# Rotated attention: transposes and values one pair later behind the scores

## The chip, the cores and the metric

The kernel runs on one core of one Trainium2 chip. Its engines are TensorE (PE, with its weight loads PEld), VectorE (DVE), ScalarE (ACT), GpSimd (POOL) and SyncE (SP, which starts the transfers). The metric is the time of one execution on the device in microseconds, lower is better; it is given as the median of three runs.

## The reference, cut to what matters

The program is a decoder: an attention layer with rotated queries and keys (stage A), a cross attention, a gated layer, six layers of linear attention, another cross attention, and six layers (stage F) of rotated local attention followed by a gated layer. The change touches the rotated local attention alone, in stage A and in the six layers of stage F. There are 2 batches of 512 tokens, 16 heads of 64, and each query sees itself and the 32 tokens before it.

```python
# stage F, one layer; stage A is the same without l2norm, scales and QK_SCALE
q = l2norm(q) * qs
k = l2norm(k) * ksc
q = q * cos * scale + rotate_half(q) * sin * scale
k = k * cos * inv + rotate_half(k) * sin * inv
mask = (it < jb) | (it > jb + w) | (jb == -1)
sim = jnp.einsum('bhwie,bhwje->bhwij', bq, bk2) * QK_SCALE
sim = jnp.where(mask, -jnp.finfo(sim.dtype).max, sim)
attn = jax.nn.softmax(sim, -1)
out = jnp.einsum('bhwij,bhwje->bhwie', attn, bv2)
return out @ Wo
```

## The kernel before, in words

Every engine has its own program, written out by hand in the order in which it is to run, and semaphores tie them. One batch of rotated attention has two parts. The first makes the projections of queries, keys and values; DVE multiplies them with the rotation's tables, SP swaps halves by a transfer, and POOL adds the two products (L559, L560). The second goes over the 8 pairs of heads, and this is where the change is. In what follows a step p is one turn of the loop over pairs on PE.

In step p PE does, in this order: a wait for the query, for the key and for both differences of pair p - 1, whose scores stand in the same two banks of PSUM; in stage F alone the spread of the norms of pair p + 1 over the partitions (L324, two matmuls); the mask (L345, for the last pair of stage F L340) and the scores (L353, 16 matmuls); the transposes of the probabilities of pair p - 1 (L367, four for each head, each head behind its own wait for POOL); and the values of pair p - 2 (L384). At step 8 the output products of pairs 0 to 3 (L394) stand ahead of the last transposes, later those of 4, 5 and of 6, 7. In steps 0 and 1 one value projection each (L276) stands among them.

DVE does for each pair the norm product of the next query (L507), the maximum of both heads (L527), the difference (L530), the sum of the exponentials (L538) and its reciprocal (L541); behind the last pair it adds the output to x (L545). ACT takes the exponential (L471), copies the norms of the next key (L455), the transposes (L478) and the values (L483). POOL multiplies the next key with its norms (L552, in stage F from pair 2 on) and then scales the probabilities with the reciprocal (L567), in the order L552 of p + 1, L567 of p, L552 of p + 2.

Probabilities lie in P, one buffer for each head and two pairs; the differences in shft, likewise; the transposes in PT, likewise. P is set to zero ahead of stage A (L1735) and ahead of stage F (L1636), since the transposes read a few columns that the exponential doesn't write. In batch 1 of a layer of stage F the parts of the next token shift and norm stand between the pairs: L1594 and L1595 on DVE behind pair 1, L1515 on PE in step 2, L1604 on DVE behind pair 3, L1188 on PE in step 4.

Of the kernel before, what the change touches and what calls it, by code (L numbers as in the profile page):

```python
# [21 lines left out]
ALU = mybir.AluOpType  # L22
ACT = mybir.ActivationFunctionType
AX = mybir.AxisListType.X
# [71 lines left out]
def build(nc, A, out, book):  # L96
    Signal.every = []
    nc.disable_value_cache = True
    with ExitStack() as c:
# [65 lines left out]
        def read(eng, bank, sgn, key):  # L165

            eng.wait_ge(*sgn.at(key))
            eng.sem_inc(free[bank].mark()[0], 1)
# [47 lines left out]
        tmp = ar(3, 2, T)  # L216
        sinp = ar(3, 2 * T)
        swp = ar(3, 2 * T)
        shft = ar(4, 384)
        P = ar(4, 640)  # L220
        PT = ar(4, 512)
        rn = rs[:, 1, :]
        knr = ar(2, T)
        ssel = ar(4, 32)
        spr = ar(4, 128)
        scl = ar(2)
# [31 lines left out]
            eng.wait_ge(swapped[n % 3], Loop.reg * per + (per + at) if Loop.now else at)  # L258

        FIRST = 2  # L260

        def k_full(key, b, p, l2):

# [2 lines left out]
        def blocks(v):  # L266
            return v.rearrange("p (j k) -> p j k", j=4)[:, :, 0:KW]
# [90 lines left out]
        def a_turn_pe(pe, key, b, p):  # L358
            for h in range(2):
                pe.wait_ge(*scaled.at((key, b, p, h)))  # L360
                if p == 0:
                    take(pe, 4 + h)
                else:
                    pe.wait_ge(*turned.at((key, b, p - 1, h)))
                for j in range(4):
                    at0 = 160 * j - (WIN if j % 2 else 0)
                    last = pe.transpose(ps[:, 4 + h, 128 * j:128 * j + 128], P[:, 2 * (p % 2) + h, at0:at0 + 128], ident[:, :])  # L367
                last.then_inc(*full[4 + h].mark((key, b, "t", p)))

        def a_values_pe(pe, key, b, p):  # L370
# [27 lines left out]
        def attn_pe(pe, key, src, l2, between={}):  # L398
            for b in range(B):
                a_proj_pe(pe, key, b, src(b), l2)  # L400
                if l2:
                    a_spread_pe(pe, key, b, 0)
                for p in range(NP + 2):
                    if p < 2:
                        a_v_pe(pe, key, b, src(b), NT + 2 + p)
                    if p < NP:
                        a_scores_wait(pe, key, b, p, l2)
                    if l2 and p + 1 < NP:
                        a_spread_pe(pe, key, b, p + 1)
                    if p < NP:  # L410
                        a_scores_pe(pe, key, b, p, l2)
                    if b == 1 and p in between:
                        between[p]()
                    if p == NP:
                        a_out_pe(pe, key, b, range(0, 4))
                    if 1 <= p <= NP:
                        a_turn_pe(pe, key, b, p - 1)
                    if p >= 2:
                        a_values_pe(pe, key, b, p - 2)
                    if p == NP:  # L420
                        a_out_pe(pe, key, b, range(4, 6))
                a_out_pe(pe, key, b, range(6, NP))

# [35 lines left out]
        def attn_act(act, key, l2, between={}):  # L459
            for b in range(B):  # L460
                a_proj_act(act, key, b, l2)
                for p in range(NP + 2):
                    if p < 2:
                        a_v_act(act, key, b, NT + 2 + p)
                    if l2 and FIRST <= p + 1 < NP:
                        a_k_norm_act(act, key, b, p + 1)
                    if p < NP:
                        for h in range(2):
                            i = 2 * (p % 2) + h
                            act.wait_ge(*subbed.at((key, b, p, h)))  # L470
                            act.activation(blocks(P[:, i, :]), shft[:, i, :].rearrange("p (j k) -> p j k", j=4), ACT.Exp,  # L471
                                           scale=8.0 if l2 else D ** -0.5).then_inc(*exped.mark((key, b, p, h)))
                    if 1 <= p <= NP:
                        for h in range(2):
                            act.wait_ge(*full[4 + h].at((key, b, "t", p - 1)))
                            if p >= 3:
                                act.wait_ge(*full[6].at((key, b, "o", p - 3)))
                            act.activation(PT[:, 2 * ((p - 1) % 2) + h, :], ps[:, 4 + h, :], ACT.Copy).then_inc(*turned.mark((key, b, p - 1, h)))  # L478
                            if p == NP:
                                read(act, 4 + h, turned, (key, b, p - 1, h))  # L480
                    if p >= 2:
                        act.wait_ge(*full[6].at((key, b, "o", p - 2)))
                        act.activation(OT[:, p - 2, :], ps[:, 6, :], ACT.Copy).then_inc(*merged.mark((key, b, p - 2)))  # L483
                        if p == NP + 1:
                            read(act, 6, merged, (key, b, p - 2))
                    if b == 1 and p in between:
                        between[p]()

# [26 lines left out]
        def attn_dve(dve, key, l2, between={}):  # L515
            for b in range(B):
                a_proj_dve(dve, key, b, l2)
                if l2:
                    a_q_norm_dve(dve, key, b, 0)
                for p in range(NP):  # L520
                    if l2 and p + 1 < NP:
                        a_q_norm_dve(dve, key, b, p + 1)
                    s4 = lambda h: ps[:, h, 0:4 * KW].rearrange("p (j k) -> p j k", j=4)
                    i = p % 3
                    for h in range(2):
                        dve.wait_ge(*full[h].at((key, b, "s", p)))
                        dve.tensor_reduce(nm[:, i, 4 * h:4 * h + 4], s4(h), AX, ALU.max).then_inc(*topped.mark((key, b, p, h)))  # L527
                    for h in range(2):
                        dve.wait_ge(*topped.at((key, b, p, h)))
                        dve.tensor_tensor(shft[:, 2 * (p % 2) + h, :].rearrange("p (j k) -> p j k", j=4), s4(h),  # L530
                                          nm[:, i, 4 * h:4 * h + 4].unsqueeze(2).to_broadcast([128, 4, KW]), ALU.subtract)\
                            .then_inc(*subbed.mark((key, b, p, h)))
                    if p == NP - 1:
                        for h in range(2):
                            read(dve, h, subbed, (key, b, p, h))
                    for h in range(2):
                        dve.wait_ge(*exped.at((key, b, p, h)))
                        dve.tensor_reduce(nm[:, i, 8 + 4 * h:12 + 4 * h], blocks(P[:, 2 * (p % 2) + h, :]), AX, ALU.add)\  # L538
                            .then_inc(*added.mark((key, b, p, h)))
                    dve.wait_ge(*added.at((key, b, p, 1)))  # L540
                    dve.reciprocal(nm[:, i, 16:24], nm[:, i, 8:16]).then_inc(*inverted.mark((key, b, p)))  # L541
                    if b == 1 and p in between:
                        between[p]()
                dve.wait_ge(*full[3].at((key, b, "y")))
                dve.tensor_tensor(x[:, T * b:T * b + T], x[:, T * b:T * b + T], ps[:, 3, :], ALU.add)\  # L545
                    .then_inc(*x_new.mark((key, b)))
                read(dve, 3, x_new, (key, b))
# [6 lines left out]
        def attn_pool(pool, key, l2):  # L554
            for b in range(B):
                for p in range(NP):
                    i = slot(b, p)
                    swap_wait(pool, b, p)
                    pool.tensor_tensor(Q[:, p, :], tmp[:, i, 0, :], swp[:, i, 0:T], ALU.add).then_inc(*roped.mark((key, b, p)))  # L559
                    pool.tensor_tensor(KT[:, p, :], tmp[:, i, 1, :], swp[:, i, T:2 * T], ALU.add).then_inc(*k_added.mark((key, b, p)))  # L560
                for p in range(NP):
                    if l2 and FIRST <= p + 1 < NP:
                        a_k_raise_pool(pool, key, b, p + 1)
                    pool.wait_ge(*inverted.at((key, b, p)))
                    for h in range(2):
                        v = blocks(P[:, 2 * (p % 2) + h, :])
                        pool.tensor_tensor(v, v, nm[:, p % 3, 16 + 4 * h:20 + 4 * h].unsqueeze(2).to_broadcast([128, 4, KW]), ALU.mult)\  # L567
                            .then_inc(*scaled.mark((key, b, p, h)))
                pool.wait_ge(*scaled.at((key, b, NP - 1, 1)))
# [37 lines left out]


        fix = sb("fix", [128, 3400])
        fat = [0]  # L610

        def keep(*dims):
# [1266 lines left out]
```

## Time and profile before

| | |
|---|---|
| median of 3 runs | 2211.46 us (2206.73 to 2217.43) |
| the profiled execution | 2206.81 us |
| its span | 2205.0 us |
| PE busy | 1757.6 us, 80% |
| DVE busy | 1332.5 us, 60% |
| ACT busy | 887.0 us, 40% |
| POOL busy | 552.3 us, 25% |
| mean granted TensorE clock | 0.881 |

The span goes from the first to the last instruction. Busy time is a mean over stages with different limits; the row of one instruction group says how long one of them took and, behind the bar, how long its engine idled ahead of it and what released it. Matmuls overlap, so the distance between the starts of two rows says more than their length. The granted clock is the share of TensorE's full speed: 1.00 is 2.4 GHz, 0.50 is 1.2 GHz.

### The profile page before, as it was taken

The numbers are of one execution on the slowest core, as the hardware profiler recorded it, in microseconds if no ns is written. First come the engines' busy times: TensorE is split into PE (matmuls) and PEld (weight loads), VectorE is DVE, ScalarE is ACT, GpSimd is POOL, SyncE is SP. The second block draws the span as 40 slices with busy tenths as digits, with TensorE's granted clock in tenths as the row PEclk, the third lists the DMA queues.
The fourth block names the chain that finished last, engine by engine and source line by source line (L and its number), as shares of the span: only waits on it lengthen the run. The fifth ranks groups of instructions, "written<-read, shape, count | busy, mean of one in ns | idle before, by whom it ended". The sixth has DMA issues, their size and how long they took to land.

```text
span 2205.0 us, 44619 instructions
## 1 busy us (share of the span) xinstructions
PE 1757.6 (80%) x15573; PEld 935.4 (42%) x15573; DVE 1332.5 (60%) x2278; ACT 887.0 (40%) x1529; POOL 552.3 (25%) x524
## 2 busy tenths in 40 slices
PE   6883331588887988886769989998988989998998
PEld 2552110254554636452225444453552543544544
DVE  6655577473544636353357748657666775685774
ACT  2341110224132241423235555454555554555545
POOL 3440000000000000000015516534543462461652
PEclk9996555698888798987779999999999999999999
DMA  5110000000000000000032313313214123132230
GB/s 201 54 59 0 0 0 0 21 6 13 7 11 8 11 17 1 17 1 0 1 113 65 104 51 104 104 40 114 79 38 140 47 62 127 27 104 82 72 104 11
DMA packets 48288, 111.26 MB, mean 50 GB/s; under 512 B 15024, under 2 KB 17840, under 8 KB 46896
## 3 DMA queue, kind: packets, MB, share of 16 engines
q1 hardware_dynamic: 48048, 108.00, 14.8%
q8 instruction: 157, 2.57, 0.5%
q14 instruction: 83, 0.68, 0.1%
HBM read 28.54 MB, written 0.52 MB: 13 GB/s over the span
## 4 chain that ended last, share of the span: by engine, by line
issue 63%; PE 17%; POOL 12%; DVE 4%; ACT 2%; DMA 1%; POOLq 0%; DVEq 0%; ACTq 0%; SPq 0%
POOL big L567 4%; POOL big L559 3%; POOL big L560 3%; PE ps L394 3%; POOL big L552 2%; PE ps L287 2%; PE ps L292 2%; PE ps L384 2%; PE ps L324 2%; PE ps L367 1%; PE ps L310 1%; PE ps L276 1%; DVE big L530 1%; PE ps L353 1%; DMA big<-big 1%
## 5 line engine op out<-in xcount | busy, mean ns | idle before, releaser
L559 POOL TENSOR_TENSOR big<-big 128x512 f32<-128x512 f32 x112 | 142.6, 1273 | 1390.3 <-DMA big<-big 1389.4
L567 POOL TENSOR_TENSOR big<-big,nm 128x384 f32<-128x384 f32 x224 | 184.3, 844 | 217.1 <-DVE nm L541 217.1
L471 ACT ACTIVATE big<-big 128x384 f32<-128x384 f32 x224 | 110.3, 523 | 211.2 <-DVE big L530 210.7
L500 DVE TENSOR_TENSOR big<-ps,big 128x512 f32<-128x512 f32 x224 | 153.5, 685 | 43.0 <-POOL big L560 26.3
L367 PE MATMUL ps<-ident,big 128*128 128x128 f32 x896 | 143.2, 294 | 30.0 <-POOL big L567 20.8
L501 DVE TENSOR_TENSOR big<-ps,big 128x512 f32<-128x512 f32 x224 | 152.1, 679 | 0.0
L560 POOL TENSOR_TENSOR big<-big 128x512 f32<-128x512 f32 x112 | 142.8, 1275 | 0.0
L324 PE MATMUL ps<-rs,big 32*128 32x512 f32 x384 | 109.9, 648 | 41.0 <-DVE big L530 20.4
L478 ACT ACTIVATE big<-ps 128x512 f32<-128x512 f32 x224 | 121.5, 585 | 50.8 <-PE ps L367 47.3
L527 DVE TENSOR_REDUCE nm<-ps 128x4 f32<-128x384 f32 x224 | 113.8, 549 | 40.4 <-PE ps L353 40.1
L1399 DVE TENSOR_TENSOR big<-ps,fix 128x512 f32<-128x512 f32 x192 | 119.4, 683 | 29.7 <-PE ps L1147 25.8
L1147 PE MATMUL ps<-big 32*128 32x128 f32 x1536 | 114.0, 340 | 27.1 <-DVE big L1399 15.6
L367 PEld LDWEIGHTS ps<-ident,big 128*128 128x128 f32 x896 | 103.8, 148 | 74.1 <-issue 49.5
L1278 ACT ACTIVATE sq<-xc 128x512 f32<-128x512 f32 x36 | 22.7, 629 | 276.4 <-DVE xc L1422 274.4
L384 PE MATMUL ps<-big 128*64 128x64 f32 x3584 | 129.0, 225 | 0.0
L1147 PEld LDWEIGHTS ps<-big 32*128 32x128 f32 x1536 | 101.4, 236 | 57.4 <-DVE big L1399 24.1
L384 PEld LDWEIGHTS ps<-big 128*64 128x64 f32 x3584 | 113.5, 138 | 27.2 <-issue 27.2
L538 DVE TENSOR_REDUCE nm<-big 128x4 f32<-128x384 f32 x224 | 113.8, 549 | 16.0 <-ACT big L471 4.1
L287 PE MATMUL ps<-xsh,big 128*128 128x512 f32 x192 | 104.1, 625 | 21.1 <-issue 15.0
L530 DVE TENSOR_TENSOR big<-ps,nm 128x384 f32<-128x384 f32 x224 | 113.2, 546 | 0.0
L427 ACT ACTIVATE big<-ps 128x512 f32<-128x512 f32 x112 | 65.1, 592 | 111.6 <-PE ps L276 111.6
L394 PE MATMUL ps<-big 128*128 128x512 f32 x224 | 107.4, 612 | 0.0
(245 smaller groups left out, 3163.9 us busy)
## 6 DMA issues: line engine op xcount, KB each, us to landing
big<-big SPq DMA_DIRECT2D x224, 256.0 KB, 2.4
big<-big SPq DMA_DIRECT2D x112, 128.0 KB, 2.4
big<-in_F_w SPq DMA_DIRECT2D x6, 1536.0 KB, 6.0
big<-big SPq DMA_DIRECT2D x84, 64.0 KB, 2.0
big<-in_D_w SPq DMA_DIRECT2D x18, 256.0 KB, 2.7
big<-in_F_wo SPq DMA_DIRECT2D x6, 512.0 KB, 7.1
big<-in_F_w SPq DMA_DIRECT2D x6, 341.0 KB, 3.0
big<-in_A_w SPq DMA_DIRECT2D x1, 1536.0 KB, 9.8
```

The costliest lines, as they stand in the source:

```text
L287: pe.matmul(ps[:, kq, :], Wqkv[:, 0, 128 * p:128 * p + 128], src, start=True, stop=True).then_inc(*full[kq].mark((key, b, "q", p)))
L324: pe.matmul(ps[:, k, :], spr[r:r + 32, p // 2, :], rn[r:r + 32, :], start=True, stop=True, tile_position=(r, 0))\
L367: last = pe.transpose(ps[:, 4 + h, 128 * j:128 * j + 128], P[:, 2 * (p % 2) + h, at0:at0 + 128], ident[:, :])
L384: last = pe.matmul(ps[64 * h:64 * h + 64, 6, 64 * m:64 * m + 64], vv[:, m // 2, 128 * p + 64 * h:128 * p + 64 * h + 64], PT[:, 2 * (p % 2) ...
L394: last = pe.matmul(ps[:, 3, :], Wo[:, p, :], OT[:, p, :], start=p == 0, stop=p == NP - 1)
L500: dve.tensor_tensor(tmp[:, i, w, :], ps[:, k, :], tb[:, 2 * w, :], ALU.mult).then_inc(*part.mark((key, b, p, 0)))
L501: dve.tensor_tensor(sinp[:, i, T * w:T * w + T], ps[:, k, :], tb[:, 2 * w + 1, :], ALU.mult).then_inc(*part.mark((key, b, p, 1)))
L530: dve.tensor_tensor(shft[:, 2 * (p % 2) + h, :].rearrange("p (j k) -> p j k", j=4), s4(h), nm[:, i, 4 * h:4 * h + 4].unsqueeze(2).to_broad ...
L559: pool.tensor_tensor(Q[:, p, :], tmp[:, i, 0, :], swp[:, i, 0:T], ALU.add).then_inc(*roped.mark((key, b, p)))
L560: pool.tensor_tensor(KT[:, p, :], tmp[:, i, 1, :], swp[:, i, T:2 * T], ALU.add).then_inc(*k_added.mark((key, b, p)))
L567: pool.tensor_tensor(v, v, nm[:, p % 3, 16 + 4 * h:20 + 4 * h].unsqueeze(2).to_broadcast([128, 4, KW]), ALU.mult)\
L1147: last = pe.matmul(ps[:, r, 128 * gp:128 * gp + 128], Kz[rows, b, gp, sl], Qf[rows, b, gp // 2, sl], start=True, stop=True, tile_position= ...
```

## The change

The transposes of pair p - 2 and the values of pair p - 3 now stand in step p, where those of p - 1 and p - 2 stood, on PE and with them the copies on ACT. The loop has one turn more. P has buffers for three pairs, shft for one. The norm copy knr lies in an unused part of another tensor, fix, so that the buffers fit. Nothing else is computed, and no transfer is changed.

```diff
-        shft = ar(4, 384)
-        P = ar(4, 640)
+        shft = ar(2, 384)
+        P = ar(6, 640)
         PT = ar(4, 512)
         rn = rs[:, 1, :]
-        knr = ar(2, T)
...
+        LATE = 2
...
-                for p in range(NP + 2):
+                for p in range(NP + LATE + 1):
...
-                    if 1 <= p <= NP:
-                        a_turn_pe(pe, key, b, p - 1)
-                    if p >= 2:
-                        a_values_pe(pe, key, b, p - 2)
-                    if p == NP:
+                    if LATE <= p < NP + LATE:
+                        a_turn_pe(pe, key, b, p - LATE)
+                    if p > LATE:
+                        a_values_pe(pe, key, b, p - LATE - 1)
+                    if p == NP + 1:
                         a_out_pe(pe, key, b, range(4, 6))
...
-                            i = 2 * (p % 2) + h
                             act.wait_ge(*subbed.at((key, b, p, h)))
-                            act.activation(blocks(P[:, i, :]), shft[:, i, :].rearrange("p (j k) -> p j k", j=4), ACT.Exp,
+                            act.activation(blocks(P[:, 2 * (p % 3) + h, :]), shft[:, h, :].rearrange("p (j k) -> p j k", j=4), ACT.Exp,
...
+        knr = fix[:, N:2 * N].rearrange("p (i t) -> p i t", i=2)
```

On PE, at the start of the pairs of stage A, batch 0, before (L345 and L353 are mask and scores of a pair, L276 a value projection, L367 transposes, L384 values):

```order
L276 MATMUL ps<-big,xn 128x512
L345 MATMUL ps<-band,identb 64x384 x4
L353 MATMUL ps<-big 64x64 x2
L353 MATMUL ps<-big 64x96 x14
L367 MATMUL ps<-ident,big 128x128 x8
L345 MATMUL ps<-band,identb 64x384 x4
L353 MATMUL ps<-big 64x64 x2
L353 MATMUL ps<-big 64x96 x14
L367 MATMUL ps<-ident,big 128x128 x8
L384 MATMUL ps<-big 64x64 x16
```

The same place in the changed kernel:

```order
L276 MATMUL ps<-big,xn 128x512
L345 MATMUL ps<-band,identb 64x384 x4
L353 MATMUL ps<-big 64x64 x2
L353 MATMUL ps<-big 64x96 x14
L345 MATMUL ps<-band,identb 64x384 x4
L353 MATMUL ps<-big 64x64 x2
L353 MATMUL ps<-big 64x96 x14
L367 MATMUL ps<-ident,big 128x128 x8
```

The scores of pair 2 have moved ahead of the first transposes, and the first values one step back. In stage F the same happens, with L324 ahead of each mask.

On PE, behind the last scores of that batch, in the changed kernel (L394 are output products, L287 is the next batch's first projection):

```order
L384 MATMUL ps<-big 64x64 x16
L394 MATMUL ps<-big 128x512 x4
L367 MATMUL ps<-ident,big 128x128 x8
L384 MATMUL ps<-big 64x64 x16
L367 MATMUL ps<-ident,big 128x128 x8
L384 MATMUL ps<-big 64x64 x16
L394 MATMUL ps<-big 128x512 x2
L384 MATMUL ps<-big 64x64 x16
L394 MATMUL ps<-big 128x512 x2
L287 MATMUL ps<-xn,big 128x512
```

Before, one group of L367 and one of L384 stood between the first and the second L394; now there are two of each.

## Rows read from the trace of the kernel before

**Rows 1.** The page's first line.
```profile
span 2205.0 us, 44619 instructions
```

**Rows 2.** Groups by line: busy, mean ns, idle before and its releaser.
```profile
L545 DVE TENSOR_TENSOR x<-x,ps 128x512 f32<-128x512 f32 x14 | 9.6, 688 | 142.8 <-PE ps L394 142.8
```

**Rows 3.** Timeline, PE, stage F mid-batch: start, us, engine, line, operation, idle before.
```profile
1720.78 1.13 PE L324 MATMUL ps<-rs,big 32*128 32x512 f32 x4
...
1724.23 1.15 PE L384 MATMUL ps<-big 128*64 128x64 f32 x32
...
1729.70 1.13 PE L324 MATMUL ps<-rs,big 32*128 32x512 f32 x4
```

**Rows 4.** Timeline, PE, the same batch behind its last pair.
```profile
1734.24 0.50 PE L340 MATMUL ps<-bandw,identb 128*128 128x384 bf16 x2
...
1736.18 1.43 PE L367 MATMUL ps<-ident,big 128*128 128x128 f32 x8 [0.62 <-POOL big L567]
...
1738.62 3.70 PE L394 MATMUL ps<-big 128*128 128x512 f32 x8
1742.16 1.04 PE L367 MATMUL ps<-ident,big 128*128 128x128 f32 x8
1743.13 1.15 PE L384 MATMUL ps<-big 128*64 128x64 f32 x32
1744.21 1.98 PE L394 MATMUL ps<-big 128*128 128x512 f32 x4
```

**Rows 5.** Timeline, all engines, steps 1 and 2 of a batch at full clock.
```profile
1534.84 1.27 POOL L552 TENSOR_TENSOR big<-big 128x512 f32<-128x512 f32 x1
1535.09 1.01 DVE L530 TENSOR_TENSOR big<-ps,nm 128x384 f32<-128x384 f32 x2
...
1536.52 1.13 PE L324 MATMUL ps<-rs,big 32*128 32x512 f32 x4 [0.86 <-POOL big L552]
...
1537.56 1.61 POOL L567 TENSOR_TENSOR big<-big,nm 128x384 f32<-128x384 f32 x2 [1.45 <-DVE nm L541]
...
1539.57 1.01 DVE L530 TENSOR_TENSOR big<-ps,nm 128x384 f32<-128x384 f32 x2
```

**Rows 6.** Timeline, a spread that waited for DVE alone.
```profile
1710.52 1.01 DVE L530 TENSOR_TENSOR big<-ps,nm 128x384 f32<-128x384 f32 x2
...
1711.76 1.23 PE L324 MATMUL ps<-rs,big 32*128 32x512 f32 x4 [0.31 <-DVE big L530]
```

**Rows 7.** Windows: busy of PE, PEld, DVE, ACT, POOL; PEclk; DMA share, GB/s.
```profile
1706.00:1709.00 3.00, 1.92 (x34) 1.15 (x38) 2.76 (x6) 2.07 (x4) 0.69 (x1) 0.93 0.07 18
1709.00:1712.00 3.00, 2.69 (x24) 2.08 (x18) 2.29 (x5) 0.90 (x3) 2.15 (x3) 0.50 0.21 44
1432.00:1435.00 3.00, 3.00 (x40) 1.43 (x36) 2.52 (x5) 1.36 (x3) 2.31 (x3) 0.50 0.02 5
```

**Rows 8.** Timeline, PE, spread and scores at half clock.
```profile
1431.49 2.08 PE L324 MATMUL ps<-rs,big 32*128 32x512 f32 x4 [0.33 <-DVE big L530]
...
1433.81 1.49 PE L353 MATMUL ps<-big 64*64 64x64 f32 x32
```

**Rows 9.** Timeline, stage A, batch 0: PE and DVE.
```profile
57.08 1.97 PE L367 MATMUL ps<-ident,big 128*128 128x128 f32 x8 [4.35 <-POOL big L567]
58.98 0.54 PE L345 MATMUL ps<-band,identb 64*64 64x384 bf16 x4
...
60.49 1.02 DVE L527 TENSOR_REDUCE nm<-ps 128x4 f32<-128x384 f32 x2 [4.35 <-PE ps L353]
...
63.73 0.97 DVE L527 TENSOR_REDUCE nm<-ps 128x4 f32<-128x384 f32 x2
...
82.82 3.70 PE L394 MATMUL ps<-big 128*128 128x512 f32 x8
```

**Rows 10.** Timeline, the start: zeroing of P, and the first norm.
```profile
1.36 2.19 DVE L1735 MEMSET big<- 128x2560 f32 x1 [1.36 <-PEq L1873]
...
7.97 0.69 DVE L185 TENSOR_TENSOR xc<-x,ps 128x512 f32<-128x512 f32 x1
```

More of the change, by code:

```diff
@@ L366, in a_turn_pe @@
                     at0 = 160 * j - (WIN if j % 2 else 0)
-                    last = pe.transpose(ps[:, 4 + h, 128 * j:128 * j + 128], P[:, 2 * (p % 2) + h, at0:at0 + 128], ident[:, :])
+                    last = pe.transpose(ps[:, 4 + h, 128 * j:128 * j + 128], P[:, 2 * (p % 3) + h, at0:at0 + 128], ident[:, :])
                 last.then_inc(*full[4 + h].mark((key, b, "t", p)))
@@ L461, in attn_act @@
                 a_proj_act(act, key, b, l2)
-                for p in range(NP + 2):
+                for p in range(NP + LATE + 1):
                     if p < 2:
@@ L468, in attn_act @@
                         for h in range(2):
-                            i = 2 * (p % 2) + h
                             act.wait_ge(*subbed.at((key, b, p, h)))
-                            act.activation(blocks(P[:, i, :]), shft[:, i, :].rearrange("p (j k) -> p j k", j=4), ACT.Exp,
+                            act.activation(blocks(P[:, 2 * (p % 3) + h, :]), shft[:, h, :].rearrange("p (j k) -> p j k", j=4), ACT.Exp,
                                            scale=8.0 if l2 else D ** -0.5).then_inc(*exped.mark((key, b, p, h)))
-                    if 1 <= p <= NP:
+                    i = p - LATE
+                    if 0 <= i < NP:
                         for h in range(2):
[L475 to L485, printed above, removed]
+                            act.wait_ge(*full[4 + h].at((key, b, "t", i)))
+                            if i >= 2:
+                                act.wait_ge(*full[6].at((key, b, "o", i - 2)))
+                            act.activation(PT[:, 2 * (i % 2) + h, :], ps[:, 4 + h, :], ACT.Copy).then_inc(*turned.mark((key, b, i, h)))
+                            if i == NP - 1:
+                                read(act, 4 + h, turned, (key, b, i, h))
+                    if i >= 1:
+                        act.wait_ge(*full[6].at((key, b, "o", i - 1)))
+                        act.activation(OT[:, i - 1, :], ps[:, 6, :], ACT.Copy).then_inc(*merged.mark((key, b, i - 1)))
+                        if i == NP:
+                            read(act, 6, merged, (key, b, i - 1))
                     if b == 1 and p in between:
@@ L529, in attn_dve @@
                         dve.wait_ge(*topped.at((key, b, p, h)))
-                        dve.tensor_tensor(shft[:, 2 * (p % 2) + h, :].rearrange("p (j k) -> p j k", j=4), s4(h),
+                        dve.tensor_tensor(shft[:, h, :].rearrange("p (j k) -> p j k", j=4), s4(h),
                                           nm[:, i, 4 * h:4 * h + 4].unsqueeze(2).to_broadcast([128, 4, KW]), ALU.subtract)\
@@ L537, in attn_dve @@
                         dve.wait_ge(*exped.at((key, b, p, h)))
-                        dve.tensor_reduce(nm[:, i, 8 + 4 * h:12 + 4 * h], blocks(P[:, 2 * (p % 2) + h, :]), AX, ALU.add)\
+                        dve.tensor_reduce(nm[:, i, 8 + 4 * h:12 + 4 * h], blocks(P[:, 2 * (p % 3) + h, :]), AX, ALU.add)\
                             .then_inc(*added.mark((key, b, p, h)))
@@ L565, in attn_pool @@
                     for h in range(2):
-                        v = blocks(P[:, 2 * (p % 2) + h, :])
+                        v = blocks(P[:, 2 * (p % 3) + h, :])
                         pool.tensor_tensor(v, v, nm[:, p % 3, 16 + 4 * h:20 + 4 * h].unsqueeze(2).to_broadcast([128, 4, KW]), ALU.mult)\
```

## The prediction

> **What bounds the kernel now.** I read, in this order, the page, the list of instruction groups, the timeline of one layer of stage F, the same stretch in the other batches, the timeline of stage A, and the granted clock in short windows. The edit touches only the rotated attention: stage A and the six layers of stage F, two batches each, so 14 batches of 8 pairs, inside a span of 2205.0 us (the execution itself took 2206.81) [rows 1].
>
> A pair of heads costs a step. In F it is, on PE, the spread of the norms (L324), the mask and the scores (L345, L353), the transposes (L367) and the values (L384); on DVE the norm product, maximum, difference, sum and reciprocal; on POOL the scaling of the probabilities (L567) and the k product (L552). In mid-batch PE runs without a gap: two steps take 1729.70 - 1720.78 = 8.92 us, and the values end just where the next L324 starts [rows 3]. Of the 8.92 about 0.4 is PE standing between the two heads' transposes, since POOL has not yet scaled the second head. So PE is the bound by a hair, with a wait on POOL in it. Behind the last pair PE waits 0.62 for POOL before the transposes of pair 6, and then runs a tail with no gap at all: output products, transposes, values, output products [rows 4]. The reader should see that DVE has nothing to do in that tail: its addition L545 waits 142.8 us in 14 batches for the last L394, 10.2 each [rows 2]. Whatever is added to the tail is paid in full.
>
> In A there is no norm and no k product. POOL is still busy with the rotations when the first probabilities are there, so PE waits 4.35 us before the first transposes, and DVE waits as long for the third pair's scores, which stand behind those transposes on PE [rows 9]. Later steps alternate between short ones and ones with a 1.2 us wait for POOL.
>
> **The change part by part.**
>
> *The tail.* Transposes of pair p - 2 and values of p - 3 now stand at step p. After the last scores PE has one set of transposes and one of values more to do. They cost 1743.13 - 1742.16 = 0.97 and 1744.21 - 1743.13 = 1.08 [rows 4], together 2.05 per batch. No wait existed there that they could fill (the one at 1736.18 stands ahead of the tail). They come out of steps 1 and 2, where PE was waiting for DVE anyway. Bounds: 2.05 whole, or 1.4 if the copies on ACT hid a part. I take 2.05.
>
> *Steps in F, batch 0.* With the transposes one step later POOL's scaling is no longer waited for directly, and PE needs 1.06 + 0.95 + 0.97 + 1.08 = 4.06 per step. What is late next? First DVE: from the start of a spread to the end of the differences is 1539.57 + 1.01 - 1536.52 = 4.06 [rows 5], and from there to the next spread 1711.76 - 1711.53 = 0.23 [rows 6]: 4.29 a step, 8.58 for two. Second POOL, which is not relieved: the k product of pair p + 1 still stands behind the scaling of pair p - 1. From the end of the differences (1536.10) the scaling starts 1.46 later, takes 1.57 to the start of L552, L552 takes 1.27, and PE starts 0.41 after its end (1536.11 to 1536.52) [rows 5]. That is 4.71, and with 4.06 on it, 8.77 for two steps. So two steps go from 8.92 to 8.77 and not to 8.58: 0.3 over four steps, and 0.2 at the last, where no spread is needed. After the last scores 1738.62 - 1734.24 = 4.38 [rows 4] becomes 1.32 for mask and scores, 0.97 and 1.08: 3.37, 1.0 less. Batch 0: -0.3 - 0.2 - 1.0 + 2.05 = +0.55.
>
> *Steps in F, batch 1.* The work put between its pairs (token shift, mean, variance, root) holds the steps open on DVE and ACT and stays. I take -0.3 (between 0 and the 0.5 of batch 0) and -0.8 after the last scores: +0.95. Six layers: 6 x (0.55 + 0.95) = +9.0; bounds +4 (all steps at 8.58) and +12 (no step shorter).
>
> *Stage A.* Scores of pair 2 now stand ahead of the first transposes. These start at 57.08 as before, for POOL's rotations are unchanged; behind them, at 58.98, come scores 3 instead of 2. From there to the output products it was 82.82 - 58.98 = 23.84. Now there are four steps at DVE's pace of 63.73 - 60.49 = 3.24 [rows 9], 3.0 for the last scores, transposes and values, and I add 1.0 for a slow clock at the start: 17.0, so -6.8, and +2.05 for the tail: -4.8 a batch, -9.6 for both. Bounds -13 and -5.
>
> *The buffers.* P grows from 4 to 6 times 640 columns. It is zeroed twice, on DVE, ahead of a norm that waits for it: the 2560 columns took 2.19, and L185 starts as soon as the zeroing is over [rows 10]. Half as much again is 1.1, twice: +2.2. One difference buffer per head costs nothing: DVE's sum of pair p - 1 has already waited for the exponential that reads it. Three buffers of P are enough, as ACT reaches the exponential of p after it copied the transposes of p - 3. The norm copy on a borrowed place in another tensor moves no instruction. No DMA moves, and SP's and POOL's queues keep their order. On ACT the copies of the transposes (L478) and of the values (L483) move with PE's work, still behind the exponential of their step, so no new wait stands ahead of an exponential.
>
> *The clock.* At the end of step 0 in F PE idles 1.40 us, as in all 12 batches, and in 8 of the 12 F batches the granted clock then falls from 1.00 (2.4 GHz) to 0.50 (1.2 GHz) in step 1; it stays there for three or four microseconds, in one batch for about ten [rows 7, 8]. In step 1 the slow transposes partly fill a gap, so a fall costs 0.3 to 1.0 us, 3.2 in the long one; over 12 batches 8 us, 0.67 each. The change takes the transposes out of step 1 and the values out of step 2. PE then idles about 2.3 us in step 1 (4.29 less 2.0 of spread and scores) and 1.3 in step 2. A clock that often fell after 1.40 will nearly always fall after both, and the slow stretch will lie on the spread and scores of step 2, which DVE waits for: 1.13 becomes 2.08 and 0.83 becomes 1.49 [rows 8], +1.6 to +1.8 a batch. Net of the 0.67 I take +1.1 x 12 = +13. Bounds: 0 (no more falls than now), and +30 if most batches do what the long one did.
>
> The Trainium skill, page "TensorE: Matmul & The Clock Gate", section "What's actually happening", says that the throttled state is the default and that activity releases it. By that rule work taken out of a thin stretch is paid again in clock, and the sum would be the one above; without it, it would be 13 less. The trace agrees: full clock through the dense tail, half clock after thin steps.
>
> **The sum.** +9.0 - 9.6 + 2.2 + 13 = +14.6 on the profiled 2206.81: 2221.4. The median of the runs, 2211.46, stands 4.65 above the profiled execution, so by it the forecast is 2226; I say 2225.
>
> **The rivals.**
> *Clock unchanged.* The falls of the clock stay at 8 in 12 with the same price. For it: four batches hold full clock through the same 1.40. Against: the gap grows. +9.0 - 9.6 + 2.2 = +1.6, 2213.
> *Faster: no waits, no falls.* The extra step of lead keeps PE from waiting on POOL, steps follow each other at DVE's 4.29, and the work ahead in A and F closes the thin stretch, so that the clock no longer falls. Then F is +4, A -13, the buffers +2.2, and the 8 us of clock come back: -15, 2197. It decides in step 1 of each F batch: no granted clock under 1.00 there. Against it stands that instructions leave this step.
> *Long falls.* PE, idle in the slow stretch too, does not get its clock back at once, and most batches look like the one at 1429 [rows 7]. Clock +28: 2240.
> *The lead does not work*, because something holds scores 2 behind the first transposes in A (a buffer of P or of the differences). Then A gives nothing, and the time is about 2235 with the clock's term. The buffers argue against it.
>
> **Chances.** Forecast 0.50, clock unchanged 0.25, long falls 0.12, no lead 0.05, faster 0.08. About 0.5% (11 us) is what a measurement of this kernel can tell from no change. Slower by more than that: most of the forecast (0.39; its own range, 2217 to 2233, reaches under 2222.5), long falls and no lead, 0.56. Faster 0.07. Same 0.37. The range is 2203 to 2239: from the clock-unchanged case with A at its best to the long falls.
>
> **What would show it.** Right: L394 starts about 5 us sooner against the first scores in A, the stretch from the first L394 to L545 is 2.05 longer in all 14 batches, two mid-batch steps take 8.8, the zeroing of P takes 3.3, and windows of 0.50 stand in steps 1 to 2 of nearly every F batch. Wrong: full clock in those steps, or a tail that did not grow, or steps at 8.6, or a first transposes' start in A other than 57 + 1.1.

## The result, and the profile after

The changed kernel takes 2227.55 us (median of 8 runs, 2222.19 to 2235.71). The kernel before, on the same chip, takes 2208.98 us (8 runs, 2199.77 to 2217.43). The ratio is 1.0085, with a 95% interval of 1.0058 to 1.0112: slower by about 0.85%. Here and in the experiments the ratio and its interval are worked out over all the runs, and are not the quotient of the two medians. The forecast was 2225 us, and its likeliest side was slower.

The profiled execution took 2223.19 us, 16.38 more than the one before; the spans differ by 16.4, so all of it can be looked for in the trace. The page of the changed kernel, its first lines (compare [rows 1]; PE was busy for 1757.6 us before, and the mean granted clock falls from 0.881 to 0.864):

```profile
span 2221.4 us, 44619 instructions
...
PE 1763.4 (79%) x15573; PEld 944.6 (43%) x15573; DVE 1335.4 (60%) x2278; ACT 891.3 (40%) x1529; POOL 553.5 (25%) x524
```

The same instructions, and yet PE is busy for 5.8 us more. The groups of the kernel before (busy us, mean ns, then the idle time ahead of them and what ended it):

```profile
L367 PE MATMUL ps<-ident,big 128*128 128x128 f32 x896 | 143.2, 294 | 30.0 <-POOL big L567 20.8
...
L324 PE MATMUL ps<-rs,big 32*128 32x512 f32 x384 | 109.9, 648 | 41.0 <-DVE big L530 20.4 <-DVE big L513 8.2 <-ACT rs L447 7.9
```

and of the changed kernel, with the addition that answers to [rows 2]:

```profile
L367 PE MATMUL ps<-ident,big 128*128 128x128 f32 x896 | 131.4, 294 | 1.1 <-POOL big L567 0.9
...
L324 PE MATMUL ps<-rs,big 32*128 32x512 f32 x384 | 123.4, 721 | 68.1 <-DVE big L530 27.7 <-POOL big L552 19.3 <-DVE big L513 8.1
...
L545 DVE TENSOR_TENSOR x<-x,ps 128x512 f32<-128x512 f32 x14 | 9.6, 688 | 158.3 <-PE ps L394 158.3
```

Three things are seen. The wait of the transposes for POOL is gone, 30.0 us down to 1.1. The wait ahead of the spread L324 has grown by 27.1 us. Its waits for DVE's difference grew by 7.3, and POOL's k product, which was not among the three largest before (so under 7.9), now ends 19.3 of it. That the two sums are nearly equal does not mean that one wait has moved: 21.3 of the 27.1 lie in one place, ahead of the third spread of each batch of F, where step 1 ends. It waited 0.31 to 0.89 us before and waits 2.21 to 2.42 now, in 8 of the 12 batches for POOL's k product (8 x 2.41 is the 19.3), in the others for DVE's difference. One of the eight:

```profile
1245.45 2.08 PE L324 MATMUL ps<-rs,big 32*128 32x512 f32 x4 [2.41 <-POOL big L552]
```

And the mean spread takes 721 ns instead of 648: the same matmuls at a lower clock. The addition behind each batch waits 15.5 us more in 14 batches. That is 1.1 a batch, and not 2.05, since the idle time ahead of L545 starts only where DVE's last work of the batch ends.

From there the span can be taken apart by the starts of a few instructions. Each row is a stretch; the numbers are from the two traces:

| stretch | before | after | difference |
|---|---|---|---|
| start to first scores of A | 48.24 | 48.48 | +0.24 |
| first scores of A to the second L545 | 112.88 | 103.14 | -9.74 |
| stages in between, up to the zeroing for F | 957.80 | 955.68 | -2.12 |
| the zeroing for F, up to the norm | 8.13 | 9.46 | +1.33 |
| norm to the first scores of F | 44.81 | 44.80 | -0.01 |
| first scores of F to the last L545 | 1006.71 | 1033.38 | +26.67 |
| last L545 to the end | 26.43 | 26.46 | +0.03 |

Stage F loses 26.7, A gives back 9.7. Within F the 12 batches, each from its first mask to L545, were summed in three pieces: the loop up to the last mask 386.9 to 400.8 (+13.9), from there to the first L394 51.3 to 40.2 (-11.1), from the first L394 to L545 127.2 to 152.5 (+25.3).

The slow clock is seen at once in a batch of F. Windows of the changed kernel (columns as in [rows 7]), over steps 0 to 3 of the batch that begins at 1524.83:

```profile
1525.00:1528.00 3.00, 1.90 (x38) 0.94 (x31) 3.00 (x6) 0.36 (x1) 0.69 (x1) 1.00 0.48 107
1528.00:1531.00 3.00, 2.28 (x40) 1.21 (x40) 2.37 (x6) 1.71 (x4) 1.47 (x2) 0.84 0.21 44
1531.00:1534.00 3.00, 1.22 (x4) 0.51 (x4) 2.78 (x7) 0.99 (x2) 1.37 (x2) 0.50 0.00 0
1534.00:1537.00 3.00, 3.00 (x41) 1.91 (x39) 1.05 (x2) 0.60 (x1) 2.88 (x3) 0.50 0.00 0
1537.00:1540.00 3.00, 2.69 (x12) 1.61 (x10) 2.81 (x7) 1.84 (x4) 0.00 (x0) 0.50 0.03 5
1540.00:1543.00 3.00, 3.00 (x42) 1.87 (x39) 1.02 (x2) 0.72 (x2) 2.81 (x3) 0.50 0.00 0
```

PEclk, the granted clock and the third value from the end of each line, falls in step 1 and is 0.50 in the last four windows, that is for at least 12 us. In the kernel before the same batch held 1.00 through all its steps, though it had the same idle 1.40 us ahead of the second spread (a row and the window around it):

```profile
1532.04 1.13 PE L324 MATMUL ps<-rs,big 32*128 32x512 f32 x4 [1.40 <-DVE big L530]
```

```profile
1531.00:1534.00 3.00, 1.96 (x40) 1.11 (x40) 2.72 (x6) 2.07 (x4) 0.73 (x1) 1.00 0.09 22
```

The place of the fall in the changed kernel, in the timeline of PE and DVE (start, us, engine, line, and in brackets the idle time before):

```profile
1528.30 1.13 PE L324 MATMUL ps<-rs,big 32*128 32x512 f32 x4 [1.40 <-DVE big L530]
...
1529.55 1.03 PE L353 MATMUL ps<-big 64*64 64x64 f32 x32
...
1532.78 2.08 PE L324 MATMUL ps<-rs,big 32*128 32x512 f32 x4 [2.21 <-DVE big L530]
...
1534.88 0.69 DVE L507 TENSOR_TENSOR big<-big,ps 128x512 f32<-128x512 f32 x1 [0.95 <-PE ps L324]
...
1535.11 1.49 PE L353 MATMUL ps<-big 64*64 64x64 f32 x32
...
1536.64 1.02 DVE L527 TENSOR_REDUCE nm<-ps 128x4 f32<-128x384 f32 x2 [1.07 <-PE ps L353]
...
1538.82 2.08 PE L324 MATMUL ps<-rs,big 32*128 32x512 f32 x4 [0.31 <-DVE big L530]
```

The gap that was 1.40 is followed by a new one of 2.21, because nothing but spread and scores is left in step 1 (before, 0.86 us were idle there). The spread that ends it runs at half clock, and DVE, which sets the pace here, waits for it twice: 0.95 us ahead of the norm product, 1.07 ahead of the maximum. So this step takes 1538.82 - 1532.78 = 6.04 us. At full clock it takes 4.29 to 4.38 (experiment 3).

The tail of the same batch, which answers to [rows 4]:

```profile
1558.10 0.50 PE L340 MATMUL ps<-bandw,identb 128*128 128x384 bf16 x2
...
1561.45 3.70 PE L394 MATMUL ps<-big 128*128 128x512 f32 x8
1564.99 1.04 PE L367 MATMUL ps<-ident,big 128*128 128x128 f32 x8
1565.96 1.15 PE L384 MATMUL ps<-big 128*64 128x64 f32 x32
1567.04 1.09 PE L367 MATMUL ps<-ident,big 128*128 128x128 f32 x8
1568.06 1.15 PE L384 MATMUL ps<-big 128*64 128x64 f32 x32
1569.14 1.98 PE L394 MATMUL ps<-big 128*128 128x512 f32 x4
```

From the first to the second L394 it is now 7.69 us; before, it was 5.59. No gap, so the additional pair is paid in full. In front of it, from the last mask to the first L394, 3.35 instead of 4.38.

Stage A, batch 0, which answers to [rows 9]:

```profile
55.15 0.36 PE L345 MATMUL ps<-band,identb 64*64 64x384 bf16 x4 [2.18 <-DVE big L530]
...
57.44 1.97 PE L367 MATMUL ps<-ident,big 128*128 128x128 f32 x8 [0.75 <-POOL big L567]
59.34 0.53 PE L345 MATMUL ps<-band,identb 64*64 64x384 bf16 x4
...
66.91 0.36 PE L345 MATMUL ps<-band,identb 64*64 64x384 bf16 x4
...
70.10 0.36 PE L345 MATMUL ps<-band,identb 64*64 64x384 bf16 x4
...
76.47 3.70 PE L394 MATMUL ps<-big 128*128 128x512 f32 x8
```

The scores of pair 2 stand ahead of the first transposes, PE waits 0.75 us for POOL instead of 4.35, and the output products begin at 76.47 instead of 82.82. The steps have DVE's pace, 70.10 - 66.91 = 3.19.

The start, which answers to [rows 10]:

```profile
1.62 3.26 DVE L1736 MEMSET big<- 128x3840 f32 x1 [1.62 <-PEq L1874]
...
9.30 0.69 DVE L185 TENSOR_TENSOR xc<-x,ps 128x512 f32<-128x512 f32 x1
```

The norm begins 1.33 us later (9.30 against 7.97).

### The profile page after: what moved, and what is told of

Read it like the earlier page. It is cut to its first block, busy times and chain, and to the rows that moved or that the text cites. A ratio compares the mean times of both kernels' runs of the same rounds, so it can differ in the third digit from the quotient of the medians.

```text
span 2221.4 us, 44619 instructions
## 1 busy us (share of the span) xinstructions
PE 1763.4 (79%) x15573; PEld 944.6 (43%) x15573; DVE 1335.4 (60%) x2278; ACT 891.3 (40%) x1529; POOL 553.5 (25%) x524
## 4 chain that ended last, share of the span: by engine, by line
issue 68%; POOL 17%; PE 8%; DVE 3%; ACT 2%; DMA 1%; POOLq 0%; ACTq 0%; SPq 0%; DVEq 0%
POOL big L559 5%; POOL big L560 5%; POOL big L567 4%; POOL big L552 3%; PE ps L324 2%; PE ps L367 1%; PE ps L353 1%; PE ps L384 1%; DMA big<-big 1%; PE ps L394 1%; DVE big L530 1%; PE ps L1516 1%; DVE big L501 1%; ACT big L478 0%; PE ps L345 0%
## 5 line engine op out<-in xcount | busy, mean ns | idle before, releaser
L324 PE MATMUL ps<-rs,big 32*128 32x512 f32 x384 | 123.4, 721 | 68.1 <-DVE big L530 27.7
L367 PE MATMUL ps<-ident,big 128*128 128x128 f32 x896 | 131.4, 294 | 1.1 <-POOL big L567 0.9
L384 PE MATMUL ps<-big 128*64 128x64 f32 x3584 | 129.7, 226 | 0.0
L384 PEld LDWEIGHTS ps<-big 128*64 128x64 f32 x3584 | 114.2, 138 | 27.1 <-issue 27.1
L367 PEld LDWEIGHTS ps<-ident,big 128*128 128x128 f32 x896 | 107.1, 151 | 28.9 <-issue 19.0
L287 PE MATMUL ps<-xsh,big 128*128 128x512 f32 x192 | 102.3, 615 | 20.9 <-issue 15.6
L353 PE MATMUL ps<-big 64*64 64x96 f32 (+1 forms) x3584 | 107.4, 261 | 0.0
```

Source lines behind the costliest of these rows:

```text
L324: pe.matmul(ps[:, k, :], spr[r:r + 32, p // 2, :], rn[r:r + 32, :], start=True, stop=True, tile_position=(r, 0))\
L353: last = pe.matmul(ps[64 * c_:64 * c_ + 64, h, KW * j + k0:KW * j + KW], Q[rows, p, 64 * m:64 * m + 64], KT[rows, p, 64 * m - WIN + k0:64 ...
L384: last = pe.matmul(ps[64 * h:64 * h + 64, 6, 64 * m:64 * m + 64], vv[:, m // 2, 128 * p + 64 * h:128 * p + 64 * h + 64], PT[:, 2 * (p % 2) ...
```

## The experiments

All are edits of the changed kernel. Two helpers serve them. The first lets each stage choose its own distance:

```diff
-        LATE = 2
+        late = {"A": 2, "F": 1}
...
         def attn_pe(pe, key, src, l2, between={}):
+            LATE = late[key]
...
-                    if p == NP + 1:
+                    if p == NP + LATE - 1:
                         a_out_pe(pe, key, b, range(4, 6))
```

The second gives PE additional work, transposes of the identity into a bank of PSUM from which nobody reads them, in the gaps of steps 0, 1 and 2. Nothing of the kernel's own work is left out:

```diff
+        def a_fill_pe(pe, key, p):
+            if key not in "F":
+                return
+            if p == 0:
+                take(pe, 5)
+            for j in range(fills[p]):
+                pe.transpose(ps[:, 5, 128 * (j % 4):128 * (j % 4) + 128], ident[:, :], ident[:, :])
...
+                    if p == 1:
+                        a_fill_pe(pe, key, 0)
...
+                    if 1 <= p <= LATE:
+                        a_fill_pe(pe, key, p)
```

The filler of step 0 stands behind the value projection, ahead of the second spread; those of steps 1 and 2 behind that step's scores. PE's wait for that bank, which stood ahead of the first transposes of the second head, moves ahead of the first filler. Experiments 5 to 8 give the numbers of fillers for each stage by itself.

In this order: are the buffers to blame (1), does A alone gain (2), what does the order cost in F without the clock (3 and 4), which gap brings the clock down (7 and 8), and is there a better kernel (5 and 6).

### 1. The buffers alone

```diff
-        LATE = 2
+        late = {"A": 1, "F": 1}
```

> The new buffers alone: P for three pairs, one difference buffer per head, the norm copy in the other tensor; transposes and values stay one and two pairs behind the scores, everywhere. If the order of work makes the difference (my theory), this is the kernel before plus the longer zeroing of P: 0 to +2 us on it, no longer tail (L394 to L545 as before, 10 us of DVE idle per batch), and the clock falls in about 8 of 12 batches of stage F as before. If the buffers themselves cost (the rival: a single difference buffer, or the norm copy's new place, holds something up), it takes +5 to +18 us.

Measured: 2214.91 us against 2213.01 before, ratio 1.0013, interval 0.9993 to 1.0034. The order is that of before, with the new buffers. The sums over F (loops, last mask to first L394, first L394 to L545) are near those of before: 384.5, 51.2 and 127.2, with 6 batches in which the clock falls instead of 8. The idle time ahead of L545 is 141.8. All of it is as expected. So three buffers of P, one of differences and the other place of the norm copy make no new wait; what is left of them is the zeroing. Ahead of F it takes 3.26 us, as in the changed kernel.

### 2. The later order in A alone

```diff
-        LATE = 2
+        late = {"A": 2, "F": 1}
```

> One pair more of delay in stage A alone, stage F in its old order, on the new buffers. My theory (stage A gains some 5 us a batch because scores of pair 2 no longer stand behind transposes that wait for POOL; stage F is where the loss is): about 10 us faster than the kernel before, ratio 0.995 to 0.997, and stage F as before. Rival (the tail and the clock cost as much in A as they bring): within 2 us of the kernel before, and the slower time of the changed kernel is spread over both stages.

Measured: 2207.87 us against 2213.01, ratio 0.9967, interval 0.9944 to 0.9990. From the first scores of A to the second L545 it is 103.33 us, in experiment 1 it was 112.85: -9.5. F is as before (385.8, 51.6, 127.2; 7 falls). A gains, F alone is where the change loses. By the medians the gain on the kernel before is 5.1 and not the 10 that were expected: the longer zeroing, 1.33 ahead of each of the two norms, was left out of the expectation. Beside experiment 1, which has it too, the medians are 7.0 apart.

### 3. The later order in both, the gaps of F filled

```diff
+        fills = {0: 8, 1: 16, 2: 8}
```

> The changed kernel with extra matmuls of the identity on PE in stage F that nothing reads: 8 ahead of the second step, 16 in step 1 and 8 in step 2 of each batch, where PE would idle. They add work and nothing else. If the clock's fall in steps 1 and 2 is what costs most in F (my theory), the granted clock stays 1.00 there and the kernel gets 20 to 29 us faster than the changed one, so 2 to 10 us faster than the kernel before; what then is left in F is the longer tail, 2.1 us a batch, less 0.9 at the last scores. If the clock is only an accompaniment and the steps are slow for another reason (the POOL chain, the missing buffer), the fillers bring nothing, or cost their 0.5 to 1 us a batch: 2227 or more.

Measured: 2205.00 us against 2213.01, ratio 0.9985 (the quotient of the medians is 0.9964), interval 0.9958 to 1.0011. Against the changed kernel's ratio of 1.0085 that is 1.0% less, some 22 us; 20 to 29 were expected. Whether it is faster than the kernel before the interval leaves open. The sums over F are 374.3, 40.2, 152.5. The loops are 26.6 us shorter than in the changed kernel, with 384 matmuls more, and the clock falls in none of the 12 batches. The windows over the end of step 0, step 1 and most of step 2 of the batch that begins at 1515.89:

```profile
1519.00:1522.00 3.00, 2.55 (x45) 1.66 (x46) 2.48 (x6) 1.77 (x4) 1.41 (x2) 1.00 0.20 42
1522.00:1525.00 3.00, 2.57 (x22) 1.58 (x23) 2.73 (x7) 0.99 (x2) 1.47 (x3) 1.00 0.01 1
1525.00:1528.00 3.00, 2.83 (x52) 2.45 (x52) 2.64 (x5) 1.12 (x3) 2.82 (x3) 1.00 0.02 5
```

and its timeline shows why the fillers (L378) cost nothing: they end before the spread has what it waits for.

```profile
1521.46 1.97 PE L378 MATMUL ps<-ident 128*128 128x128 f32 x16
1523.86 1.13 PE L324 MATMUL ps<-rs,big 32*128 32x512 f32 x4 [0.43 <-DVE big L546]
...
1525.86 1.09 PE L378 MATMUL ps<-ident 128*128 128x128 f32 x8
...
1528.23 1.13 PE L324 MATMUL ps<-rs,big 32*128 32x512 f32 x4 [0.41 <-DVE big L546]
```

### 4. The earlier order in both, the gaps of F filled

```diff
+        late = {"A": 1, "F": 1}
...
+        fills = {0: 8, 1: 4, 2: 0}
```

> The old order in both stages (on the new buffers) with 8 unread matmuls ahead of the second step and 4 in step 1 of each batch of stage F. My theory: the 8 falls of the clock in the kernel before cost 8 us in all (0.67 a batch), so this is 6 to 8 us faster than the kernel before. The difference of this kernel to the one with both stages late and filled is then the order alone at full clock: about 0.5 to 1 us a batch dearer in F for the late order (+9), 10 us cheaper in A, so the two within 3 us of each other. If the falls before cost nothing, it is within 1 us of the kernel with the buffers alone.

Measured: 2198.26 us against 2213.01, ratio 0.9945, interval 0.9922 to 0.9967. The sums over F are 378.6, 51.9, 127.2. In each of the two kernels the loops of the first batches are alike to 0.1 us, and those of the second too, with no batch that stands out; so the two beside each other give the price of the order in F alone:

| F, 12 batches | early (4) | late (3) | difference |
|---|---|---|---|
| loops | 378.6 | 374.3 | -4.4 |
| last mask to first L394 | 51.9 | 40.2 | -11.7 |
| first L394 to L545 | 127.2 | 152.5 | +25.3 |
| sum | 557.8 | 567.0 | +9.2 |

And each beside its unfilled kernel gives the price of the clock: 26.6 in the changed kernel, and (386.9 + 51.3) - (378.6 + 51.9) = 7.7 before. The 7.7 is of one execution; experiments 1 and 2, which have the same order in F, give 5.2 and 6.8 in the same way.

The medians do not bear out this price. The expectation was that this kernel would be 6 to 8 us faster than the one before and within 3 us of experiment 3. It is 14.8 faster (by the interval 7 to 17), and 6.7 faster than experiment 3, where F's +9.2 and A's -9.7 make -0.5. The profiled execution, 2206.24, was the slowest of its nine, so its trace can't say where the others are shorter. That stays open, and the price of the order in F rests on the rows of these two traces.

### 5. Late in A, early in F, the gaps of F filled

```diff
+        late = {"A": 2, "F": 1}
...
+        fills = {'F': (8, 4, 0)}
```

> Late order in stage A, old order in stage F, with 8 unread matmuls ahead of the second step and 4 in step 1 of each F batch. If the two gains are independent (my theory: 10 us from the order in A, about 8 to 12 from the clock in F), it is 17 to 22 us faster than the kernel before, ratio 0.990 to 0.993, and the F loops sum to 379 as in the old order filled. Rival: one gain eats the other (the clock's windows shift, or the gain in A is lost in the stages between): 10 to 13 us.

Measured: 2189.20 us against 2208.70 before, ratio 0.9921, interval 0.9888 to 0.9954. From the first scores of A to the second L545 103.26, the sums over F 378.6, 51.9, 127.2. What helped apart helps together, as expected.

### 6. The same, and the gaps of A filled too

```diff
+        fills = {'A': (8, 16, 8), 'F': (8, 4, 0)}
```

> The same with 8, 16 and 8 unread matmuls in the first three steps of both batches of stage A as well. The pair loops of A took 25.0 and 24.0 us with clock falls in them. If it is the clock there too, they go to about 23.5 and 23 and the kernel gains 2 to 3 us more; if the wait for POOL's rotations is the bound of those steps, nothing changes but noise.

Measured: 2180.18 us against 2208.70, ratio 0.9870, interval 0.9842 to 0.9898: the fastest of all, faster than both kernels. In A it is now 99.00 us from the first scores to the second L545, 4.3 less than in experiment 5, 2.2 of it in the two loops (23.10 and 22.65) and nearly all the rest between the first and the second of them. The clock does not fall in either. Step 3 shows it: in the changed kernel the mask at 59.34 took 0.53 and the step at half clock 4.42 us; here (kernel of experiment 6)

```profile
56.62 1.09 PE L378 MATMUL ps<-ident 128*128 128x128 f32 x8
57.99 1.44 PE L367 MATMUL ps<-ident,big 128*128 128x128 f32 x8 [0.28 <-POOL big L583]
59.36 0.36 PE L345 MATMUL ps<-band,identb 64*64 64x384 bf16 x4
...
62.51 0.36 PE L345 MATMUL ps<-band,identb 64*64 64x384 bf16 x4
```

the step takes 3.15. The medians differ by 9.0 from experiment 5, where 2 to 3 were expected; A shows 4.3 of it. The profiled execution (2191.76) was the slowest of its six and had two batches of F that began at half clock, so it can't say where the rest is. That stays open.

### 7. The changed kernel, step 0 of F alone filled

```diff
+        fills = {'F': (8, 0, 0)}
```

> The changed kernel with the 8 unread matmuls ahead of the second step of each F batch only; the gaps of steps 1 and 2 stay open. My theory (the gap that the change opens in step 1 brings the clock down by itself): the granted clock still falls in nearly all 12 batches, a step later, and the F loops sum to 390 to 402 against 400.9 in the changed kernel. Rival (it is still the old 1.40 us gap of step 0 that starts the fall, and the new gaps only prolong it): few falls are left and the loops sum to 374 to 382.

Measured in a single run: 2215.12 us, clock 0.867. The loops of F take 391.1, that is 16.8 more than filled (390 to 402 were expected). The batch that begins at 1524.91:

```profile
1526.82 1.04 PE L378 MATMUL ps<-ident 128*128 128x128 f32 x8
1528.46 1.13 PE L324 MATMUL ps<-rs,big 32*128 32x512 f32 x4 [0.61 <-DVE big L546]
...
1532.85 1.53 PE L324 MATMUL ps<-rs,big 32*128 32x512 f32 x4 [2.31 <-DVE big L546]
```

```profile
1531.00:1534.00 3.00, 1.15 (x4) 0.30 (x4) 2.74 (x7) 0.99 (x2) 1.46 (x3) 0.91 0.01 1
1534.00:1537.00 3.00, 3.00 (x43) 2.39 (x42) 1.53 (x3) 0.60 (x1) 2.82 (x3) 0.52 0.00 0
```

The gap of 1.40 is down to 0.61 and the clock falls nonetheless, a step later, behind the gap of 2.31 that the change makes. It falls in all 12 batches, and all 12 loops are longer than their filled ones, by 0.3 to 4.8 us.

### 8. The changed kernel, steps 1 and 2 of F alone filled

```diff
+        fills = {'F': (0, 16, 8)}
```

> The changed kernel with 16 and 8 unread matmuls in steps 1 and 2 of each F batch only; the 1.40 us gap of step 0 stays, as it was in the kernel before. My theory: what the change added to the clock's cost goes, what was there before stays: the clock falls in about 8 of 12 batches, and the F loops sum to 374 + 8 = 380 to 385. Rival (step 0's gap alone costs this much in the late order, since the slow scores now stand in DVE's way): 390 or more.

Measured in a single run: 2203.27 us, clock 0.879. The loops of F take 378.7, 4.4 more than filled, and the clock falls in 5 of the 12 batches, the only ones lengthened by more than 0.3 us. Both are a little less than expected (380 to 385, about 8). In the batch that begins at 1516.82 the old gap is there and the clock holds (timeline, then window):

```profile
1520.29 1.13 PE L324 MATMUL ps<-rs,big 32*128 32x512 f32 x4 [1.40 <-DVE big L546]
```

```profile
1525.00:1528.00 3.00, 3.00 (x51) 2.10 (x50) 2.49 (x7) 0.60 (x1) 2.19 (x3) 1.00 0.03 5
...
2053.00:2056.00 3.00, 1.96 (x40) 1.18 (x40) 2.72 (x6) 2.07 (x4) 0.73 (x1) 0.97 0.00 1
2056.00:2059.00 3.00, 3.00 (x21) 2.78 (x14) 2.56 (x6) 0.99 (x2) 2.12 (x3) 0.50 0.21 44
```

The other two windows are of a batch that falls, though step 1 is dense: the 1.40 us alone can do it, but does so in some batches only. Together: the gap of step 0 alone costs 4.4, those of steps 1 and 2 alone 16.8, all of them 26.6. The 5.4 that are left come only when both are there, as far as single executions tell: the same order in F, unfilled, differed by 2.5 us between three executions (7.7, 5.2, 6.8).

## Why the prediction was right, and where it was off

The forecast of the change was +14.6; in the profiled executions it was +16.4, between the medians of 8 runs +18.6. Term by term, with what measured it:

| term | predicted | measured | by |
|---|---|---|---|
| order in F, at full clock | +9.0 | +9.2 | experiments 3 and 4 |
| stage A | -9.6 | -9.7 | trace; -9.5 by experiments 1 and 2 |
| zeroing of P | +2.2 | +1.6 (0.24 and 1.33) | trace |
| clock in F | +13 | +18.9 (26.6 less 7.7) | experiments 3 and 4 against the unfilled kernels |
| anything else | 0 | -3.6 | trace |

That the sum came so near is in part luck. The clock cost 5.9 more than forecast, and against it stood 3.6 in stretches that the change does not touch and 0.6 in the zeroing. The 2225 came near the median of 2227.55 also because the median of three runs that it starts from, 2211.46, was 2.5 above that of eight.

*The tail.* 2.05 was worked out from one group of transposes and one of values; the stretch from the first L394 to L545 went from 10.60 to 12.71 in all 14 batches, 2.11 each. The bound of 1.4, by which ACT would have hidden a part, did not come into it.

*The steps.* The forecast was that DVE's pace of 4.29 would not be reached, as POOL's k product still stands behind the scaling, and that two steps take 8.77. The full steps of batch 0 take 4.29 and 4.50 in the changed kernel, together 8.79. Behind the last scores 3.37 was predicted and 3.35 measured. For the second batch of a layer the forecast was more of a choice than a reading, -0.3 and -0.8; experiments 3 and 4 give -0.14 for its loop (32.82 to 32.68 in most layers) and -0.83.

*Stage A.* The first transposes of A start at 57.44, and not at 57 + 1.1. The forecast had named that as a sign that it is wrong. The first scores are only 0.24 us later than before, and from them to the first transposes it is 8.96 us, 8.84 before, so PE still gets to them when POOL is through, as the forecast had it. The zeroing did shift the norm by 1.33, but in this execution one of the norm's pairs of matmuls ran at full clock (L180, 1.12 us instead of the 2.07 of before), and the next one came 0.95 less behind it. That is luck of the clock: in experiment 1, with the same buffers, all of them took 2.07 or more, and its first scores came 1.3 later than before, at 49.56. So the term was right in mechanism, 0.23 too small each time, since the zeroing of P itself also began 0.26 later (1.62 against 1.36; ahead of F 0.25), and partly hidden in the profiled execution. From the first scores to the output products batch 0 of A went from 34.58 to 27.99, -6.6; -6.8 was predicted (among its signs the prediction says "about 5", which takes the longer tail off, though the tail lies behind L394).

*The clock.* This is the term that was mis-sized, +13 for +18.9. Its mechanism holds: the step in the prediction was that work taken out of thin steps leaves gaps behind which the clock falls nearly always. All 12 batches fell, 8 before (6 and 7 in experiments 1 and 2). The new gap is 2.21 to 2.42 us, 2.3 was predicted. Experiment 7 shows that with the old gap cut to 0.6 the new ones still bring the clock down in all 12, experiment 3 that filling all of them takes it all back. By the forecast all falls together cost 12 x (0.67 + 1.1) = 21.2; they cost 26.6. The error was to price one slow spread and one slow set of scores, those of step 2. In batch 0 of a layer, beside experiment 3, a batch loses 3.3 on average, because the slow stretch reaches over steps 1, 2 and often 3: 5.43, 6.03, 5.43 where filled steps take 4.40, 4.38, 4.41. In batch 1 it loses 1.1, less than the forecast, because the token shift and the norm hold step 2 open anyway (5.24 filled, 5.2 to 5.8 unfilled). So what was wrong is the length of the slow stretch. By the granted clock in the traces the loops of F stood at 0.50 for 34.1 us before, 4.3 in each of 8 batches, and for 112.6 after, 9.4 in each of 12. A microsecond at half clock cost nearly the same in both, 7.7 / 34.1 = 0.23 and 26.6 / 112.6 = 0.24. The cost of the falls before was read right, 8 us against 7.7 measured. The idle time of 1.40 that the prediction gives for all 12 batches is 1.49 in the first.

The Trainium skill, page "TensorE: Matmul & The Clock Gate", section "What's actually happening", has the throttled state as the default, which activity has to release. The traces agree: 0.50 through 1531 to 1543 in a batch with gaps, 1.00 through the same steps when 32 unread transposes were put in them.

*What remains.* -2.1 lie in the stages between A and F and -1.5 between the batches of F, neither of which the change touches; among the profiled executions of all nine kernels after the change the stretch between A's second L545 and F's first scores varies between 1006.1 and 1016.8 us with the same instructions. So a term of one or two microseconds can't be read off a span, only off its own rows.

*The rivals.* "Clock unchanged" (2213) is refuted: the clock falls in 12 batches instead of 8. Its price without the clock's term is the changed kernel less the 18.9, about 2209; no run has the later order with the falls of before, and experiment 3 has none at all. "Faster" is refuted by the same windows, and its prices were not met either: A gave -9.7 and not -13, the order in F cost +9.2 and not +4. It was right only in that full clock in F (26.6) is worth more than the order costs there, and for that it needs the fillers. "Long falls" was right in part: batch 0 of four layers loses 3.5 to 4.8, that of the other two 1.8 and 2.4, and batch 1 of a layer 0.9 to 1.7; with +18.9 the clock's term lies between the forecast's 13 and this rival's 28 (its terms add up to 2241, above the upper end of the range). "The lead does not work" is refuted by the 0.75 us wait in A and by A's 9.7; its 2235 left out that A's tails would still have grown, by 2.1 each.

## What to carry to other kernels

More lead is paid at the end of every batch and earned at its start: before moving work later, see whether the start really waits (A: 4.35 us in one place) or has what it needs (F), and choose per stage. Work that stands in thin steps also keeps the matmul engine's clock up; where it leaves, look at the granted clock of those steps and price not one slow instruction but every step until 1.00 is back (here 0.23 to 0.24 us for each microsecond at 0.50). Where a gap can't be closed, cheap work that nobody reads can be put in it, as long as it ends before the next real instruction is ready: here it took back 26.6 us in F, and with the order chosen per stage and fillers in both stages the kernel is 1.3% faster than the one before (0.9842 to 0.9898).

## What the runs showed of the hardware

The clock did not follow single gaps. With the same order in F, the idle 1.40 us of step 0 was followed by a fall in 8 of 12 batches in one execution and in 6 and 7 in two others; in 5 of 12 with a dense step behind it; and in none of the 12 where it had been cut to 0.5 or 0.6 and the steps behind were filled, nor in the 24 of experiments 4 and 5, where a gap of 0.9 to 1.1 followed. Once down, the clock stayed at 0.50 for at least 12 us in a batch in which PE was busy for most of the time (windows of 3.00, 2.69 and 3.00 busy of 3 us, all at 0.50): the busy time is of slow matmuls, and a gap of 0.31 us lay between them. Half clock costs little where PE has slack, and it costs most where another engine waits for a short PE result: here 0.95 and 1.07 us of DVE's time in one step of 6.04.
